# Second layer of a fused network: keys and k by k scores of two batches ahead of all query work

## The chip, the cores and the metric

The kernel runs on one core of one Trainium2 chip. Its time is the device time of one execution in microseconds (us). Three runs of the kernel before are shown: 820.59 us (median), 819.68 and 837.18.

The core has five engines that run side by side, each through its own list of instructions in a fixed order: TensorE (PE, matmuls, with the weight load PEld beside it), VectorE (DVE), ScalarE (ACT), GpSimd (POOL) and SyncE (SP, which here only issues DMAs). They meet through semaphores. TensorE writes to PSUM, eight banks that the other engines read and free.

## The reference

x is 4 batches of 256 tokens by 256 channels. Two layers; each is an attention and a feed-forward network, both on a gated input and added to x. The change touches the attention of the second layer alone. With 16 heads of 16 channels it computes, cut to what matters:

```python
q, k = _rope(q, k)                          # q, k, v, beta from hidden_states
s = einsum('bihd,bjhd->bhij', k, k) * scale # k by k scores, strictly lower
m = max(s, -1); e = where(strict, exp(s - m), 0)
p = e / sum(e, -1)
A = p * beta + eye                          # lower triangular, 256 by 256 a head
u = solve_triangular(A, v, lower=True)
sc = einsum('bihd,bjhd->bhij', q, k) * scale
o = softmax(where(causal, sc, -inf)) @ u
return o @ Wo
```

The triangular system needs keys, values and beta; queries come in only with the last softmax. The feed-forward network behind it routes tokens to eight experts.

## The kernel before, in words

Every engine walks one list of steps, ORDER, made by make_order() (VectorE walks DVE_ORDER, the same list with some steps put a little later by lag()). A step is a tuple, such as ("proj", 1, b, 1): projection in layer 1, batch b, of keys (1) or queries (0). So the place of a step in the list sets the order on each engine; there is no planner. The steps of the second attention for batch b, with the lines of the instructions in the trace:

- gate: tanh on ScalarE (L1273), product on VectorE (L1557): the attention's input.
- proj: fp32 matmuls, then rotary embedding on VectorE (L1575 to L1578). split: three bf16 parts of the result (VectorE, L1587 to L1595), stored to DRAM by SP; for keys SP then loads two stacks, "k" and "kq" (keys in the place of queries); the step qload loads the stack "q".
- vproj: values and beta (TensorE; ScalarE L1298; VectorE L1738).
- kscores, five groups: k by k scores (TensorE), maxima (VectorE L1609 to L1618), exponential with sum (ScalarE L1350). kmax: the maxima are transposed (L1015) and written by four DMAs into the stack (SP, L832). kdiag, den, blocks: diagonal blocks of 32 by 32, transposed (L1760) for GpSimd. kprobs, four groups: the blocks below the diagonal (TensorE, ScalarE L1335).
- On GpSimd, blocks also stands for the inversion of the diagonal blocks: L1985, then 31 pairs of L1992 and L1994. It starts when VectorE has done blocks and the transpose (L1769, step inverse) of the inverse of the batch before.
- solve and update, eight and seven rounds of two halves: the block substitution. A solve is 16 small matmuls and a copy (L1791), an update is 16 matmuls (L1119) and L1777 and L1780 on VectorE. Each waits for the one before: TensorE, VectorE, TensorE.
- scores, eight groups: q by k scores (TensorE), maxima (VectorE L1628, L1629). minus, max: their transposition. probs, eight groups: scores again with the maxima in, exponential (ScalarE L1319, L1320). pv: times u. otr, oT, wo: normalisation and output projection.

proj, vproj, kscores, kdiag, kprobs, scores, probs, pv and others take turns on the two slots of the ring "mid" in PSUM (table RINGS, which also names the engine that frees each slot); a step takes the slot that the step two places before it in that ring has freed.

The list has a part ahead of the first inverse, and four substitutions. spread() deals the steps in ahead[b] (work on other batches) evenly between the rounds of substitution b. Before the change the first part does keys and queries of batches 0, 1 and 2, both batches' k by k scores, and all of batch 0's scores and probs.

## Time and profile before

| | |
|---|---|
| median of the runs | 820.59 us |
| profiled execution, its time | 820.95 us |
| its span | 819.1 us |
| VectorE busy | 555.0 us, 68% |
| TensorE busy | 515.0 us, 63% |
| ScalarE busy | 300.3 us, 37% |
| GpSimd busy | 227.1 us, 28% |
| second attention, from the first requant to its last gate | 313.47 to 650.90 us |

A row of the timeline is start, duration, engine, line, operation, output and input, count, and in brackets how long the engine had been idle before it and who released it. Times are counted from the start of the span. PEclk is the granted clock of TensorE as a share of its full speed. SPq is SP's DMA issue.

### The profile page before, as it was taken

The numbers are of one execution on the slowest core, as the hardware profiler recorded it, in microseconds if no ns is written. First come the engines' busy times: TensorE is split into PE (matmuls) and PEld (weight loads), VectorE is DVE, ScalarE is ACT, GpSimd is POOL, SyncE is SP. The second block draws the span as 40 slices with busy tenths as digits, with TensorE's granted clock in tenths as the row PEclk, the third lists the DMA queues.
The fourth block names the chain that finished last, engine by engine and source line by source line (L and its number), as shares of the span: only waits on it lengthen the run. The fifth ranks groups of instructions, "written<-read, shape, count | busy, mean of one in ns | idle before, by whom it ended". The sixth has DMA issues, their size and how long they took to land. (4 is left out here: it accounts for less than half of the span.)

```text
span 819.1 us, 17908 instructions
## 1 busy us (share of the span) xinstructions
PE 515.0 (63%) x7444; PEld 424.2 (52%) x7444; DVE 555.0 (68%) x1066; ACT 300.3 (37%) x716; POOL 227.1 (28%) x320
## 2 busy tenths in 40 slices
PE   0362555875859554327565676678886750899980
PEld 0352444764648443325443455466655540899980
DVE  6899699797969847766656684663664165667834
ACT  3354333543456340062654204523213150365520
POOL 3000000000000000104848807816830036043254
PEclk9875775986888786755586666687979555899996
DMA  8445041050000100760070150020001162666224
GB/s 307 149 76 116 1 89 28 1 117 1 2 0 2 52 0 17 159 136 5 3 155 6 40 90 7 7 47 7 10 10 12 55 245 85 245 204 235 78 58 136
DMA packets 52067, 61.30 MB, mean 75 GB/s; under 512 B 25409, under 2 KB 45393, under 8 KB 47505
## 3 DMA queue, kind: packets, MB, share of 16 engines
q1 hardware_dynamic: 50176, 55.15, 25.1%
q0 software_dynamic: 1808, 4.99, 2.0%
q8 instruction: 59, 0.97, 0.5%
q14 instruction: 24, 0.19, 0.1%
HBM read 45.24 MB, written 13.63 MB: 72 GB/s over the span
## 5 line engine op out<-in xcount | busy, mean ns | idle before, releaser
L888 PE MATMUL psum<-arena 32*32 32x16 f32 (+18 forms) x5608 | 357.6, 274 | 214.3 <-DVE arena L1557 75.7
L888 PEld LDWEIGHTS psum<-arena 32*32 32x32 f32 (+6 forms) x5608 | 284.4, 128 | 287.1 <-DVE arena L1557 78.4
L1994 POOL TENSOR_TENSOR arena<-arena 128x31 f32<-128x31 f32 (+15 forms) x124 | 68.4, 552 | 9.7
L1992 POOL TENSOR_TENSOR arena<-arena 128x31 f32<-128x31 f32 (+15 forms) x124 | 64.4, 519 | 9.7
L1350 ACT ACTIVATE psum<-psum,arena 128x256 f32<-128x256 f32 (+7 forms) x128 | 45.7, 364 | 30.4 <-DVE arena L1618 30.2
L1527 DVE TENSOR_TENSOR_SCAN arena<-arena 128x255 f32<-128x255 f32 x64 | 42.5, 726 | 11.4 <-ACT arena L1262 11.4
L1628 DVE TENSOR_REDUCE arena<-psum 128x2 f32<-128x512 f32 (+1 forms) x48 | 41.3, 861 | 12.5 <-PE psum L888 11.8
L1972 POOL DMA_DIRECT2D arena<-wq x1 | 0.9, 862 | 171.9 <-PE psum L888 171.9
L1319 ACT ACTIVATE arena<-psum 128x512 f32<-128x512 f32 (+1 forms) x48 | 35.4, 736 | 35.8 <-PE psum L888 35.5
L2005 POOL TENSOR_TENSOR fc_second_parts<-arena,fc_first_parts 128x2048 fp32r<-128x2048 f32 x6 | 27.9, 4650 | 63.7 <-ACT fc_first_parts L1438 63.7
L1262 ACT ACTIVATE arena<-arena 128x255 f32<-128x255 f32 x64 | 27.2, 498 | 46.6 <-DVE arena L1513 46.6
L1425 ACT ACTIVATE psum<-psum,arena 128x256 f32<-128x256 f32 x64 | 24.8, 457 | 48.3 <-PE psum L888 48.3
L1438 ACT ACTIVATE fc_first_parts<-arena 128x2048 fp32r<-128x2048 f32 x16 | 30.4, 1918 | 26.3 <-PE psum L888 26.3
L1119 PE MATMUL psum<-arena 32*32 32x224 f32 (+6 forms) x896 | 38.3, 317 | 2.0 <-issue 1.8
L2012 POOL DMA_INDIRECT dispatched<-arena x16 | 20.3, 1266 | 69.1 <-DVE arena L1845 64.5
L1513 DVE TENSOR_TENSOR_SCAN arena<-arena 128x256 f32<-128x256 f32 x64 | 39.0, 671 | 0.5
L888 PE MATMUL psum<-input_first_parts,fc_first_parts 128*128 128x256 f32 x128 | 37.2, 291 | 2.6 <-DVE input_second_parts L1880 1.5
L888 PE MATMUL psum<-fc_first_parts,hidden_first_parts 128*128 128x256 f32 x128 | 36.9, 288 | 2.7 <-DVE hidden_second_parts L1898 2.7
L888 PE MATMUL psum<-input_second_parts,fc_first_parts 128*128 128x256 f32 x128 | 36.8, 287 | 0.0
L888 PE MATMUL psum<-input_first_parts,fc_second_parts 128*128 128x256 f32 x128 | 36.8, 287 | 0.0
L1777 DVE STREAM_TRANSPOSE arena<-psum 128x64 f32<-128x64 f32 x56 | 13.8, 246 | 33.5 <-PE psum L1119 32.7
L888 PE MATMUL psum<-fc_first_parts,hidden_second_parts 128*128 128x256 f32 x128 | 36.2, 283 | 0.0
(179 smaller groups left out, 928.0 us busy)
## 6 DMA issues: line engine op xcount, KB each, us to landing
arena<-fc SPq DMA_DIRECT2D x16, 1024.0 KB, 5.2
arena<-parts SPq DMA_DIRECT2D x40, 256.0 KB, 4.5
parts<-arena SPq DMA_DIRECT2D x16, 384.0 KB, 3.6
arena<-parts SPq DMA_DIRECT2D x40, 128.0 KB, 5.4
dispatched<-arena SPq DMA_DIRECT2D x1, 2048.0 KB, 18.9
arena<-arena SPq DMA_DIRECT2D x128, 8.0 KB, 1.8
arena<-dispatched SPq DMA_DIRECT2D x8, 256.0 KB, 3.3
expert_rows<-arena SPq DMA_DIRECT2D x8, 256.0 KB, 2.3
```

The source lines that it names most:

```text
L888: return nc.tensor.matmul(out, lhsT, rhs, start=start, stop=stop)
L1119: last = nc.tensor.matmul(acc(half)[rows, qq, (s + 1) * BLK:T], ublk[rows, s, q, :], later[b % 2][s][rows, q, :], start=s == 0 and qq == 0 ...
L1262: A(scan[s + 1][:, ct, 0:T - 1], scan[s][:, ct, 0:T - 1], ACT.Copy, scale=back[:, i:i + 1]).then_inc(scaled, 1)
L1319: step_(A(prob[:, hs, 0:T], hi, ACT.Exp, scale=scale))
L1350: ins = A(s_, s_, ACT.Exp, bias=nbias[:, n:n + 1], accum_out=ncc[b][:, n:n + 1])
L1438: A(w_parts[i][e % 2][0][:], fcw[e % NW][i], ACT.Copy).then_inc(w_first, 1)
L1513: ins = V.tensor_tensor_scan(scan[s][:, ct, :], dd, src[:, ct, bt(b)], 0.0, ALU.mult, ALU.add)
L1527: st(V.tensor_tensor_scan(scan[s][:, ct, T - 2::-1], dd, scan[s + 1][:, ct, T - 2::-1], scan[s][:, ct, T - 1:T], ALU.mult, ALU.add))
L1628: st(V.tensor_reduce(mneg[:, H + j * n:H + (j + 1) * n], hi, axis=AX.X, op=ALU.max, negate=True))
L1992: link(G_.tensor_tensor(tmp, A3[:, k + 1:BLK, k:k + 1].to_broadcast([P, rows, w]), X3[:, k:k + 1, 0:w].to_broadcast([P, rows, w]), ALU.mult))
L1994: ins = G_.tensor_tensor(X3[:, k + 1:BLK, 0:w], X3[:, k + 1:BLK, 0:w], tmp, ALU.add)
L2005: G_.tensor_tensor(second[:], fcw[e % NW][1], first[:].bitcast(F32), ALU.subtract).then_inc(w_second[1], 1)
```

## The change

It rewrites the list. Ahead of the first inverse now stand keys and values of batches 0 and 1, k by k scores, diagonal blocks and kprobs of both (interleaved), the keys of batch 2, and behind them the queries and query scores of batch 0 and the query projection of batch 1. Batch 0's probabilities and batch 2's queries go into substitution 0, batch 3's queries into substitution 1. The step inverse stands at the end of the work dealt into the substitution before. Two waits follow: SP's load of the second "kq" stack waits for two requants in place of four, and GpSimd's fill of the third key stack stands at the first vproj.

```diff
-    o += [("requant", 0), ("gate", 2, 0)] + keys_then_queries(0) + [("qload", 0), ("vproj", 0), ("requant", 1), ("gate", 2, 1)]
-    o += keys_then_queries(1) + [("qload", 1), ("vproj", 1), ("requant", 2), ("requant", 3), ("gate", 2, 2)]
-    o += groups("kscores", 1, 0) + [("kmax", 1, 0)] + groups("scores", 1, 0)[:4] + [("kdiag", 0), ("den", 0), ("blocks", 0)]
-    o += groups("kprobs", 1, 0) + groups("scores", 1, 0)[4:] + [("minus", 1, 0), ("max", 1, 0)]
-    o += groups("kscores", 1, 1) + [("kmax", 1, 1)] + keys_then_queries(2)
-    o += [("kdiag", 1), ("den", 1), ("blocks", 1)] + groups("kprobs", 1, 1) + groups("probs", 1, 0) + [("qload", 2), ("vproj", 2)]
+    def keys(b):
+        return [("proj", 1, b, 1), ("split", 1, b, 1)]
+
+    def asked(b):
+        return [("proj", 1, b, 0), ("split", 1, b, 0)]
+
+    ks, sc, pr = ([groups(kind, 1, b) for b in range(B)] for kind in ("kscores", "scores", "probs"))
+    o += [("requant", 0), ("gate", 2, 0)] + keys(0) + [("vproj", 0), ("requant", 1), ("gate", 2, 1), ("proj", 1, 1, 1)]
+    o += ks[0][:2] + [("split", 1, 1, 1)] + ks[0][2:] + [("kmax", 1, 0), ("requant", 2), ("requant", 3), ("vproj", 1)]
+    o += [("kdiag", 0), ("den", 0), ("blocks", 0), ("gate", 2, 2)] + ks[1][:1] + groups("kprobs", 1, 0)[:2] + ks[1][1:2] + groups("kprobs", 1, 0)[2:]
+    o += ks[1][2:] + [("kmax", 1, 1)] + asked(0) + [("qload", 0)] + [("kdiag", 1), ("den", 1), ("blocks", 1)]
+    o += groups("kprobs", 1, 1) + keys(2) + sc[0] + [("minus", 1, 0), ("max", 1, 0)] + asked(1) + [("qload", 1), ("vproj", 2)]
...
-    ahead = [k2 + [[("gate", 2, 3)], [("proj", 1, 3, 1), ("split", 1, 3, 1)]] + d2 + [[("proj", 1, 3, 0), ("split", 1, 3, 0)], [("vproj", 3)]]
-             + queries(1),
-             k3 + [[("otr", 1, 0)]] + d3 + p1[:3] + [[("oT", 1, 0)]] + p1[3:6] + out(0)[1:] + p1[6:] + [[("qload", 3)]] + queries(2),
...
+    ahead = [one_each(pr[0][:4]) + k2 + [[("gate", 2, 3)]] + one_each(pr[0][4:]) + [keys(3)] + d2 + [asked(2), [("qload", 2), ("vproj", 3)]] + queries(1) + [[("inverse", 1)]],
+             k3 + [[("otr", 1, 0)]] + d3 + p1[:3] + [[("oT", 1, 0)]] + p1[3:6] + out(0)[1:] + p1[6:] + [asked(3), [("qload", 3)]]
+             + queries(2) + [[("inverse", 2)]],
...
+    o += [("inverse", 0)]
...
-        solve = [[("inverse", b), ("solve", b, 0, 0), ("solve", b, 0, 1)]]
+        solve = [[("solve", b, 0, 0), ("solve", b, 0, 1)]]
...
-                                sp.wait_ge(x_ready, 2 * B)
+                                sp.wait_ge(x_ready, B + 2)
...
-                elif kind == "qload" and step[1] == 0:
-                    pool.wait_ge(parts_ready[0], B + 1)
+                elif kind == "vproj" and step[1] == 0:
+                    pool.wait_ge(parts_ready[1], B + 1)
```

The changed file is seven lines longer ahead of the programs, so its lines are seven higher. Three places, in the order of one engine's instructions. First VectorE behind the first gate and key projection of the attention. Before, the split of the keys and then projection (L1575 to L1578) and split of the same batch's queries:

```order
L1595 TENSOR_TENSOR arena<-arena 128x512
L1575 TENSOR_TENSOR arena<-psum,arena 128x512
L1577 TENSOR_TENSOR psum<-psum,arena 128x512
L1578 TENSOR_TENSOR arena<-arena,psum 128x512
L1587 CAST arena<-arena 128x512
```

With the change, from batch 1's gate (L1564) and key projection (L1582 to L1585) on:

```order
L1564 SCALAR_TENSOR_TENSOR arena<-arena 128x2x256
L1582 TENSOR_TENSOR arena<-psum,arena 128x512
L1584 TENSOR_TENSOR psum<-psum,arena 128x512
L1585 TENSOR_TENSOR arena<-arena,psum 128x512
L1616 TENSOR_REDUCE arena<-psum 128x4
L1622 TENSOR_SCALAR arena<-arena 128x4
```

The first k by k scores (L1616) stand right behind the second key projection; before, two query projections, their splits and three requants came first.

Second, TensorE at the start of substitution 0. Before, behind the solve (32x16) come the k by k scores of batch 2 and then the first update (L1119):

```order
L888 MATMUL psum<-arena 32x16 x16
L888 MATMUL psum<-arena 32x256 x4
L888 MATMUL psum<-arena 32x32 x4
...
L1119 MATMUL psum<-arena 32x224 x16
L888 MATMUL psum<-arena 32x32 x32
```

With the change, behind the solve come one group of batch 0's probabilities (128x256, 128x128), the update (L1126), two groups, the next solve, one group and only then k by k scores:

```order
L895 MATMUL psum<-arena 32x16 x16
L895 MATMUL psum<-arena 128x256
L895 MATMUL psum<-arena 128x128
L895 MATMUL psum<-arena 128x256
L895 MATMUL psum<-arena 128x128 x5
L1126 MATMUL psum<-arena 32x224 x16
```

The k by k scores of batch 2 moved behind the first update; before, the first group stood ahead of it.

Third, VectorE in substitution 1, behind the update of round 4. Before, the output's residual (L1670), a gate, the solve's copy (L1791), the next update:

```order
L1780 SCALAR_TENSOR_TENSOR arena<-arena 128x16 x2
L1670 TENSOR_TENSOR arena<-psum,arena 128x2x256
L1557 SCALAR_TENSOR_TENSOR arena<-arena 128x2x256
L1791 COPY arena<-psum 128x2x16 x2
L1777 STREAM_TRANSPOSE arena<-psum 128x64
```

With the change, the copy (L1798), then projection and split of batch 3's queries and one group of scores (L1635, L1636) ahead of the next update:

```order
L1787 SCALAR_TENSOR_TENSOR arena<-arena 128x16 x2
L1798 COPY arena<-psum 128x2x16 x2
L1582 TENSOR_TENSOR arena<-psum,arena 128x512
L1584 TENSOR_TENSOR psum<-psum,arena 128x512
L1585 TENSOR_TENSOR arena<-arena,psum 128x512
L1594 CAST arena<-arena 128x512
L1599 TENSOR_TENSOR arena<-arena 128x512
L1600 CAST arena<-arena 128x512
L1602 TENSOR_TENSOR arena<-arena 128x512
L1635 TENSOR_REDUCE arena<-psum 128x2
L1636 TENSOR_REDUCE arena<-psum 128x2
L1784 STREAM_TRANSPOSE arena<-psum 128x64
```

The pair of projection and split came here from substitution 0; the residual and gate now lie one round earlier.

## Rows read from the trace of the kernel before

**Rows 1.** Stretches between inverse transposes: length; PE, PEld, DVE, ACT, POOL busy; PEclk; DMA.

```profile
313.47:428.12 114.65, 62.72 (x1571) 48.90 (x1571) 74.91 (x143) 44.37 (x169) 41.01 (x67) 0.64 0.38 81
428.12:491.45 63.33, 40.78 (x1081) 29.19 (x1081) 46.13 (x124) 14.31 (x68) 37.72 (x65) 0.66 0.27 50
491.45:556.48 65.03, 45.98 (x1198) 33.99 (x1198) 37.94 (x111) 26.02 (x93) 36.51 (x65) 0.71 0.12 19
556.48:600.73 44.25, 36.60 (x806) 27.77 (x806) 24.84 (x83) 12.70 (x27) 37.01 (x65) 0.81 0.08 9
600.73:650.90 50.17, 36.59 (x713) 26.09 (x713) 17.56 (x67) 11.53 (x23) 0.74 (x1) 0.81 0.07 8
```

**Rows 2.** Waits, 313 to 651 us: who for whom, us in total, times, longest.

```profile
POOL arena L1985 <- DVE arena L1769: 53.0, 3, 23.5
...
DVE arena L1738 <- ACT arena L1298: 8.6, 1, 8.6
```

**Rows 3.** Timeline of GpSimd: starts of the first, second and last inversion.

```profile
378.00 1.91 POOL L1985 TENSOR_TENSOR arena<-arena 128x1024 f32<-128x1024 f32 x1 [44.84 <-DVEq L1762]
...
430.20 1.91 POOL L1985 TENSOR_TENSOR arena<-arena 128x1024 f32<-128x1024 f32 x1 [9.01 <-DVE arena L1769]
...
558.62 1.91 POOL L1985 TENSOR_TENSOR arena<-arena 128x1024 f32<-128x1024 f32 x1 [23.45 <-DVE arena L1769]
```

**Rows 4.** Timeline of VectorE, 339 to 461 us.

```profile
339.70 0.69 DVE L1575 TENSOR_TENSOR arena<-psum,arena 128x512 f32<-128x512 f32 x1 [3.62 <-PE psum L888]
...
344.25 0.69 DVE L1575 TENSOR_TENSOR arena<-psum,arena 128x512 f32<-128x512 f32 x1
...
375.77 0.21 DVE L1759 STREAM_TRANSPOSE arena<-arena 128x32 f32<-128x32 f32 x1 [1.81 <-ACT arena L1328]
...
379.92 0.69 DVE L1628 TENSOR_REDUCE arena<-psum 128x2 f32<-128x512 f32 x1 [2.07 <-PE psum L888]
...
386.71 1.22 DVE L1609 TENSOR_REDUCE arena<-psum 128x4 f32<-128x1024 f32 x1 [1.51 <-PE psum L888]
...
405.37 0.69 DVE L1575 TENSOR_TENSOR arena<-psum,arena 128x512 f32<-128x512 f32 x1 [4.18 <-PE psum L888]
...
410.90 0.69 DVE L1575 TENSOR_TENSOR arena<-psum,arena 128x512 f32<-128x512 f32 x1
...
427.77 0.26 DVE L1738 TENSOR_TENSOR arena<-psum,arena 128x16 f32<-128x16 f32 x2 [8.63 <-ACT arena L1298]
...
460.55 0.34 DVE L1791 COPY arena<-psum 128x32 f32<-128x32 f32 x2 [4.31 <-PE psum L888]
```

**Rows 5.** Stretch of batch 0's k by k exponentials (L1350): length, ScalarE busy, PEclk.

```profile
354.00:368.60 14.60, 11.89 (x64) 0.50 0.61 138
```

**Rows 6.** Groups by line, ScalarE: kprobs' exponentials; busy us, mean ns, idle before.

```profile
L1335 ACT ACTIVATE arena<-psum 128x896 f32<-128x896 f32 (+6 forms) x28 | 14.9, 597 | 5.1 <-PE psum L888 5.1
```

**Rows 7.** Timeline of TensorE's matmuls, 372 to 614 us.

```profile
372.53 2.81 PE L888 MATMUL psum<-arena 98*32 98x32 bf16 x152 [0.34 <-DMA arena<-arena]
...
391.18 1.26 PE L888 MATMUL psum<-arena 96*32 96x64 bf16 x64 [3.40 <-ACT psum L1350]
...
416.80 5.14 PE L888 MATMUL psum<-arena 98*128 98x256 bf16 x40 [0.30 <-ACT arena L1335]
422.21 1.51 PE L888 MATMUL psum<-arena 98*128 98x256 bf16 x16 [0.27 <-ACT arena L1320]
...
431.15 3.13 PE L1119 MATMUL psum<-arena 32*32 32x224 f32 x32
...
452.05 2.36 PE L1119 MATMUL psum<-arena 32*32 32x160 f32 x32
...
606.90 1.72 PE L1119 MATMUL psum<-arena 32*32 32x224 f32 x32 [0.24 <-DVE arena L1791]
...
613.84 1.29 PE L1119 MATMUL psum<-arena 32*32 32x160 f32 x32
```

**Rows 8.** Timeline of SP: the four DMAs of batch 0's key maxima.

```profile
368.68 2.31 SPq L832 DMA_DIRECT2D arena<-arena  x4
```

More of the change, by code:

```diff
@@ L274, in make_order @@
     (k2, d2), (k3, d3) = inverted(2), inverted(3)
-    ahead = [k2 + [[("gate", 2, 3)], [("proj", 1, 3, 1), ("split", 1, 3, 1)]] + d2 + [[("proj", 1, 3, 0), ("split", 1, 3, 0)], [("vproj", 3)]]
-             + queries(1),
-             k3 + [[("otr", 1, 0)]] + d3 + p1[:3] + [[("oT", 1, 0)]] + p1[3:6] + out(0)[1:] + p1[6:] + [[("qload", 3)]] + queries(2),
-             [[("otr", 1, 1)]] + p2[:3] + [[("oT", 1, 1)]] + p2[3:6] + out(1)[1:] + p2[6:] + queries(3),
+    ahead = [one_each(pr[0][:4]) + k2 + [[("gate", 2, 3)]] + one_each(pr[0][4:]) + [keys(3)] + d2 + [asked(2), [("qload", 2), ("vproj", 3)]] + queries(1) + [[("inverse", 1)]],
+             k3 + [[("otr", 1, 0)]] + d3 + p1[:3] + [[("oT", 1, 0)]] + p1[3:6] + out(0)[1:] + p1[6:] + [asked(3), [("qload", 3)]]
+             + queries(2) + [[("inverse", 2)]],
+             [[("otr", 1, 1)]] + p2[:3] + [[("oT", 1, 1)]] + p2[3:6] + out(1)[1:] + p2[6:] + queries(3) + [[("inverse", 3)]],
              [[("otr", 1, 2)]] + p3[:3] + [[("oT", 1, 2)]] + p3[3:6] + out(2)[1:] + p3[6:]]
+    o += [("inverse", 0)]
     for b in range(B):
-        solve = [[("inverse", b), ("solve", b, 0, 0), ("solve", b, 0, 1)]]
+        solve = [[("solve", b, 0, 0), ("solve", b, 0, 1)]]
         for s in range(1, NS):
@@ L317, in lag @@
         chain = step[0] in ("inverse", "update", "solve", "den", "blocks")
-        if step[0] == "inverse":
+        if step[0] == "solve":
             solving = True
```

## The prediction
> **What bounds the kernel now.** I read the stages first. Cut at the four transposes that hand an inverse from GpSimd to the substitution (L1769), the second layer's attention takes 114.65 us up to the first, then 63.33, 65.03, 44.25 and 50.17 us [rows 1]. In none of the first three is one engine full: VectorE is busy for 74.9 of 114.65 us and 46.1 of 63.33, TensorE less, and the granted clock is 0.64, 0.66 and 0.71, so TensorE is mostly at the lower of its two levels. It is a chain that hops between engines.
>
> Then the waits: GpSimd waits 53.0 us in all for L1769 [rows 2]. Its first inverse runs from 378.00 to 421.19 (430.20 less 9.01 of waiting), 43.2 us, and it starts each of the next only when VectorE has come to the transpose in its own order; the last starts at 558.62 [rows 3] and is done as the last transpose starts at 600.73. So GpSimd binds in one stage, 556.48 to 600.73, with 44.25 us. Before that, an earlier inverse is worth nothing by itself: what counts is when VectorE reaches its transposes, at 428.12, 491.45 and 556.48. I therefore forecast those three times; the two stages behind them keep their length, since what the change does there is to swap neighbours.
>
> Last, VectorE's own idle time ahead of 428.12. The largest is 8.63 us at 427.77: TensorE and ScalarE do the eight probability groups of batch 0 and the value projection, and VectorE has nothing. Others: 3.62 us for a projection at 339.70, 1.81 and 2.07 around the diagonal blocks, 1.51 at 386.71, 4.18 at 405.37 [rows 4].
>
> **Stage A, up to the first transpose.** What goes: the 8.6 us behind the probabilities; two waits of 2.1 us in the query scores (one is the 2.07), because all eight groups now stand together with k scores, projections and diagonal long issued; the 1.5 us at 386.71; 3.3 us inside the k scores of batch 0 and before the third key projection, since a split (half of the 4.55 us of a pair, below) now lies inside the first, and part of the 4.18 is hidden at the second. That is 17.6 us. One projection and split (batch 2's queries) leave the stage; from 405.37 to 410.90 [rows 4] such a pair took 5.5 us beside a running inverse. (From 339.70 to 344.25, with GpSimd idle, 4.55.)
>
> What comes: (a) the k scores of batch 1. Now they run from 386.71 to 401.19 (405.37 less 4.18), 14.5 us. ScalarE needs 11.9 us for five such groups, eight blocks of 1.5 [rows 5], and TensorE already waits 3.40 us for it at 391.18 [rows 7], because only two slots of the middle ring exist. The change puts the four kprobs of batch 0 into the same ring between them, each one or two activations of 0.6 us [rows 6], and about as much of TensorE. Walked with these durations (VectorE's part of a group some 2.5 us, then ScalarE's 3.0, then a kprobs, then the slot), the nine steps take 22.3 us, so +7.8. (b) The diagonal of batch 0 now has only two requants and a value projection before it. Its rows are issued by 368.68 and TensorE starts 3.85 us later [rows 7, 8]; with kdiag (most of the 2.81 us of that row) and ScalarE's exponential (about 1) behind it VectorE waits 4.3 us in place of 1.81: +2.5. (c) Both query projections were hidden under the keys' split; alone, each is a wait like the 3.62 or 4.18 at a key projection [rows 4]. I take 3.2 and 3.3: +6.5. (d) The first k scores stand right behind a projection while their stack is loaded: +0.5. Sum +17.3.
>
> So idle time is a draw (-0.3), and with the work that leaves (5.5, less 0.9 that the split of batch 0's queries gains in length, since it now runs beside the inverse as the pair at 405.37 did) stage A is **4.9 us** shorter. Bounds: all of the 8.6 and 5.5 kept (14.1); nothing kept (0).
>
> **Stage B, first substitution.** In: eight probability groups, on TensorE and ScalarE. VectorE's work is the same: batch 2's queries come in, batch 3's go out. Now the first three rounds hide under k scores of batch 2; the gate is done 28.1 us after the transpose (460.55 less 4.31), the copy before the next projection 32.4 us after [rows 4]. With the change the k scores come to VectorE only behind the second update, by my walk some 8 us later, so the first two rounds have nothing on VectorE to cover them. Walked: the gate is done at 32.7 (+4.6). Then round three runs with four probability groups before the projection (at 416.80 five such took 5.14 us [rows 7], 4.1 for four, of which 2 are hidden; solve, update and VectorE's part some 3 more): the projection reaches VectorE 7.5 us later. Behind it one update and solve are missing, -1.5. Sum **+6.0**. The ends are 0 (all in holes of TensorE: it is busy 40.8 of 63.3 us [rows 1]) and 8 x 1.03 = +8.2, or 10 if the projection behind them also waits for its slot. I take the walk, which lies between.
>
> **Stage C, second substitution.** Comes in: batch 3's query projection and split. VectorE's part is 4.55 us with GpSimd idle, as it is there by then (the third inverse takes 43 of the 65 us). TensorE does the projection ahead of the solve that VectorE waits for, 2 to 3 us in which VectorE has only an update left; against that, the update behind is ready when the split ends, about -1.5. **+5.5**, ends 4 and 7.6. SP's new load of batch 3's queries waits for batch 1's last probabilities, which are issued ahead of it, and nobody needs it for 40 us: 0.
>
> **Sum.** -4.9 + 6.0 + 5.5 = +6.6 on the profiled execution's 820.95 us: 827.5. The runs shown have their median 0.36 lower: **827 us**.
>
> **A rule against the sum.** The granted clock is 0.64 to 0.71 up to 556.48 and 0.81 behind it, and prices follow: the first update takes TensorE 3.13 us in substitution 0 and 1.72 in substitution 3, the third 2.36 and 1.29, a probability group 1.03 at 416.80 and 0.75 at 422.21 [rows 1, 7]. If more work in the substitution raised the clock there, the three long updates (second one estimated between: 1.3) would give back 3.8, eight groups 2.2, two projections (by halves of a 3.6 us wait) some 1.8: 7.8 us in all, and the time would be 819. That is rival 2. The Trainium skill, "TensorE: Matmul & The Clock Gate", section "Part 1: The HAM clock gate", says just this: the throttled clock is the default, and activity releases it. By that rule the time is 819, by my rows of today's clock 827; the trace agrees with the rule in that the clock did rise within the block of probabilities, yet there nothing interrupted it, and in the substitution each group is followed by a wait.
>
> **Rivals.** Changes under 2% (16.4 us) can hardly be told from none here.
> 1. *The idle time is really gone*, 20%. The middle ring is no obstacle, stage A gives 14.1 us; B costs 0, C 4.5: -9.6, **811 us**. For it: VectorE is the engine with most work and the hole of 8.6 us is real. Against: the ring's waits for ScalarE [rows 7].
> 2. *The clock rises in stage B*, 18%: **819 us**. For it: the rise at 422.21. Against: above.
> 3. *Exposed probabilities*, 11%: slower. In stage B TensorE's order puts one or two groups before each update, and each waits for a ring slot that ScalarE frees late, as its k scores of batch 2 take 2.9 us a group. Then all rounds stretch: B +10, C +7.6, A gives nothing: +17.6, **838 us**. It decides once VectorE's idle time in stage B passes 27 us (it is 17.2, 63.33 less 46.13). For it: ScalarE is in strict order and gets 16 more activations there. Against: the first four groups come before any k scores.
> 4. *Nothing moves* (the order says otherwise: first k scores ahead of the second split) 1%.
>
> The forecast has 50%. Range 8 in 10: from 811, rival 1's sum, to 836, the forecast with B at 8.2 and C at 7.6 and A at -1 (+14.8); it leaves out rival 3 and the half of rival 1 below its sum. Chances: faster by over 2% (under 804.2) needs more than rival 1's full sum, 3%; slower by over 2% (over 837.0) rival 3, 10%; within, 87%.
>
> **What would show it.** In the profile after: first inverse starts near 362 in place of 378.00 and it changes nothing; VectorE reaches the first L1769 (now seven lines on) at 423, the next at 492 to 493, the third at 563; the k scores of batch 1 stretch over 22 us; the idle time before the first value beta (8.63) is gone; between the first transpose and the end of the gate 32 to 33 us; a projection wait of 2 to 3 us in the second substitution. I am wrong if stage A ends before 418 (rival 1), if stage B is under 64 us at a granted clock over 0.75 (rival 2), or if stages D and E change by over 2 us.

## The result, and the profile after

The changed kernel takes **829.99 us** (median of 4 runs, 826.39 to 833.2) against 820.17 us for the kernel before in the same comparison (also 4 runs): ratio 1.012, 95% interval [1.0068, 1.0173]. It is slower by some 10 us, under 2%. The profiled execution took 829.61 us, with a span of 827.8 us. The forecast was 827.0 us, range 811 to 836. Ratios rest on fast executions alone: one of 837.18 us among the four of the kernel before, and one of 1207.97 us among the six with the kprobs together below, are left out of them.

The stretches of the profile after, cut at the same instructions as [rows 1] (first requant, the four inverse transposes, last gate). The columns are length; PE, PEld, DVE, ACT, POOL busy; PEclk; DMA share; GB/s.

```profile
311.58:426.84 115.26, 56.82 (x1499) 43.58 (x1499) 69.49 (x135) 37.14 (x153) 41.64 (x67) 0.62 0.31 64
426.84:492.78 65.94, 44.21 (x1145) 33.13 (x1145) 46.95 (x123) 21.21 (x84) 37.74 (x65) 0.70 0.35 72
492.78:564.39 71.61, 50.87 (x1206) 37.56 (x1206) 42.13 (x118) 25.79 (x93) 36.56 (x65) 0.67 0.13 24
564.39:609.36 44.97, 36.70 (x805) 27.82 (x805) 24.35 (x83) 12.71 (x27) 37.45 (x66) 0.80 0.08 9
609.36:659.59 50.23, 35.20 (x713) 25.03 (x713) 17.58 (x68) 11.52 (x23) 0.26 (x1) 0.82 0.08 8
```

| stretch | before | after | difference | forecast |
|---|---|---|---|---|
| A, up to the first transpose | 114.65 | 115.26 | +0.6 | -4.9 |
| B, substitution 0 | 63.33 | 65.94 | +2.6 | +6.0 |
| C, substitution 1 | 65.03 | 71.61 | +6.6 | +5.5 |
| D and E | 94.42 | 95.20 | +0.8 | 0 |
| all | 337.43 | 348.01 | +10.6 | +6.6 |

The whole span grew by 8.7, because the first requant came 1.9 us earlier, which the change does not touch. In the kernels built from the changed one below, and in its second profile, it came between 311.5 and 313.4 us, so that is scatter. Stage A has 5.4 us less of VectorE's work than before (69.49 against 74.91) and yet is not shorter: its idle time on VectorE rose from 39.7 to 45.8 us.

VectorE's timeline in stage A, after. Columns as in the rows ahead of the prediction: start, duration, line, operation, and in brackets the idle time before it and its releaser.

```profile
338.44 1.22 DVE L1616 TENSOR_REDUCE arena<-psum 128x4 f32<-128x1024 f32 x1 [2.70 <-PE psum L895]
...
362.66 0.21 DVE L1766 STREAM_TRANSPOSE arena<-arena 128x32 f32<-128x32 f32 x1 [4.69 <-ACT arena L1335]
...
371.95 1.29 DVE L1616 TENSOR_REDUCE arena<-psum 128x4 f32<-128x128 f32 x2 [4.23 <-PE psum L895]
...
379.36 1.29 DVE L1616 TENSOR_REDUCE arena<-psum 128x4 f32<-128x256 f32 x2 [5.24 <-PE psum L895]
...
392.02 0.69 DVE L1582 TENSOR_TENSOR arena<-psum,arena 128x512 f32<-128x512 f32 x1 [4.16 <-PE psum L895]
...
402.36 0.69 DVE L1582 TENSOR_TENSOR arena<-psum,arena 128x512 f32<-128x512 f32 x1 [1.45 <-PE psum L895]
...
408.68 0.69 DVE L1635 TENSOR_REDUCE arena<-psum 128x2 f32<-128x512 f32 x1 [1.62 <-PE psum L895]
...
421.96 0.69 DVE L1582 TENSOR_TENSOR arena<-psum,arena 128x512 f32<-128x512 f32 x1 [3.57 <-PE psum L895]
...
426.51 0.26 DVE L1745 TENSOR_TENSOR arena<-psum,arena 128x16 f32<-128x16 f32 x2
426.86 1.91 DVE L1776 STREAM_TRANSPOSE arena<-arena 128x1024 f32<-128x1024 f32 x1
```

What the reader is to see: the value beta (L1745) ahead of the transpose has no idle time in front, where it had 8.63 us [rows 4]. But two waits of 4.23 and 5.24 us now stand inside the k scores of batch 1, three waits (4.16, 1.45, 3.57) stand ahead of projections that are no longer paired, and 4.69 us stand ahead of the diagonal's transpose. The hole was not closed; it was cut up.

GpSimd, after: the starts of its first, second and last inversion.

```profile
364.83 2.46 POOL L1992 TENSOR_TENSOR arena<-arena 128x1024 f32<-128x1024 f32 x1 [38.09 <-DVEq L1769]
...
428.94 1.91 POOL L1992 TENSOR_TENSOR arena<-arena 128x1024 f32<-128x1024 f32 x1 [20.29 <-DVE arena L1776]
...
566.54 1.91 POOL L1992 TENSOR_TENSOR arena<-arena 128x1024 f32<-128x1024 f32 x1 [29.95 <-DVE arena L1776]
```

The first inversion starts 13.2 us earlier than in [rows 3] (11.3 us earlier, counted from the first requant), and GpSimd then waits 20.29 us, where it waited 9.01. Its waits for the transpose add up to 73.4 us, against 53.0 [rows 2].

### The profile page after: what moved, and what is told of

The parts are those of the page before. It is cut to its first block and busy times, and to the rows that moved or that the text cites. A ratio compares the mean times of both kernels' runs of the same rounds, so it can differ in the third digit from the quotient of the medians.

```text
span 827.8 us, 17909 instructions
## 1 busy us (share of the span) xinstructions
PE 516.4 (62%) x7444; PEld 425.8 (51%) x7444; DVE 554.3 (67%) x1066; ACT 299.8 (36%) x716; POOL 227.3 (27%) x320
## 5 line engine op out<-in xcount | busy, mean ns | idle before, releaser
L895 PE MATMUL psum<-arena 32*32 32x16 f32 (+17 forms) x5608 | 356.3, 277 | 224.2 <-DVE arena L1564 71.2
L895 PEld LDWEIGHTS psum<-arena 128*32 128x32 f32 (+6 forms) x5608 | 282.4, 130 | 297.0 <-DVE arena L1564 73.2
L1357 ACT ACTIVATE psum<-psum,arena 128x256 f32<-128x256 f32 (+7 forms) x128 | 45.8, 375 | 35.8 <-DVE arena L1625 34.3
L1534 DVE TENSOR_TENSOR_SCAN arena<-arena 128x255 f32<-128x255 f32 x64 | 42.5, 726 | 11.3 <-ACT arena L1269 11.3
L1635 DVE TENSOR_REDUCE arena<-psum 128x2 f32<-128x512 f32 (+1 forms) x48 | 41.3, 861 | 10.6 <-PE psum L895 10.0
L1992 POOL TENSOR_TENSOR arena<-arena 128x1024 f32<-128x1024 f32 x4 | 8.2, 2048 | 111.5 <-DVE arena L1776 73.4
L1126 PE MATMUL psum<-arena 32*32 32x224 f32 (+6 forms) x896 | 37.7, 318 | 1.1 <-DVE arena L1798 1.1
```

The source lines that it names most:

```text
L895: return nc.tensor.matmul(out, lhsT, rhs, start=start, stop=stop)
L1126: last = nc.tensor.matmul(acc(half)[rows, qq, (s + 1) * BLK:T], ublk[rows, s, q, :], later[b % 2][s][rows, q, :], start=s == 0 and qq == 0 ...
L1357: ins = A(s_, s_, ACT.Exp, bias=nbias[:, n:n + 1], accum_out=ncc[b][:, n:n + 1])
L1534: st(V.tensor_tensor_scan(scan[s][:, ct, T - 2::-1], dd, scan[s + 1][:, ct, T - 2::-1], scan[s][:, ct, T - 1:T], ALU.mult, ALU.add))
L1635: st(V.tensor_reduce(mneg[:, H + j * n:H + (j + 1) * n], hi, axis=AX.X, op=ALU.max, negate=True))
```

## The experiments

Each was timed beside the kernel before on the same chip; ratios are to that kernel. Stage lengths are of the profiled executions.

### Only the probabilities inside

From the kernel before: batch 0's eight probability groups go into substitution 0, and behind them the load of batch 2's queries (qload), which stood behind them before; nothing else.

```diff
-    o += [("kdiag", 1), ("den", 1), ("blocks", 1)] + groups("kprobs", 1, 1) + groups("probs", 1, 0) + [("qload", 2), ("vproj", 2)]
+    o += [("kdiag", 1), ("den", 1), ("blocks", 1)] + groups("kprobs", 1, 1) + [("vproj", 2)]
-    ahead = [k2 + [[("gate", 2, 3)], [("proj", 1, 3, 1), ("split", 1, 3, 1)]] + d2 + ...
+    p0 = one_each(groups("probs", 1, 0))
+    ahead = [p0[:4] + k2 + [[("gate", 2, 3)]] + p0[4:] + [[("qload", 2)], [("proj", 1, 3, 1), ("split", 1, 3, 1)]] + d2 + ...
```

> The kernel before with one part of the change: batch 0's eight probability groups inside substitution 0 (four ahead of batch 2's k by k scores, four behind the gate), the rest of the list as before. If the hole of 8.6 us ahead of the first transpose is real and substitution 0 takes the groups as cheaply as in the changed kernel (65.94 us in place of 63.33), stage A falls to 106 us, stage B rises to 66, and the time is about 814 us (-6). Rival, the groups are exposed in the substitution (my forecast's +6.0 to +8.2): B 69.5 to 71.5, time 818 to 820.

Measured: **813.86 us**, ratio 0.9931 [0.9907, 0.9954]. Stage A takes 108.04 us (-6.6), B 65.57 (+2.2), C 64.77. Its windows A and B, and VectorE's end of stage A:

```profile
313.50:421.54 108.04, 56.91 (x1507) 44.87 (x1507) 74.98 (x142) 37.59 (x153) 40.94 (x67) 0.61 0.35 77
421.54:487.11 65.57, 42.59 (x1145) 31.61 (x1145) 47.74 (x123) 21.11 (x84) 37.60 (x65) 0.76 0.33 64
```

```profile
421.21 0.26 DVE L1739 TENSOR_TENSOR arena<-psum,arena 128x16 f32<-128x16 f32 x2 [2.11 <-ACT arena L1299]
421.56 1.91 DVE L1770 STREAM_TRANSPOSE arena<-arena 128x1024 f32<-128x1024 f32 x1
```

The 8.63 us hole shrinks to the 2.11 us of the value projection, and eight groups in the substitution cost 2.2. That is 4.4 us of the 6.8 that its second attention is shorter by. Another 2.0 lie in stage E (48.17 us, 50.17 before), where no step moved; E lies between 47.8 and 51.9 us in the profiles of the other experiments, and I did not trace why. This part of the change is a gain of its own, and what loses time in the changed kernel is elsewhere.

### The probabilities taken out again

From the changed kernel: the same step back.

```diff
-    ... + asked(1) + [("qload", 1), ("vproj", 2)]
+    ... + asked(1) + [("qload", 1)] + pr[0] + [("vproj", 2)]
-    ahead = [one_each(pr[0][:4]) + k2 + [[("gate", 2, 3)]] + one_each(pr[0][4:]) + [keys(3)] + d2 + ...
+    ahead = [k2 + [[("gate", 2, 3)]] + [keys(3)] + d2 + ...
```

> The changed kernel with batch 0's eight probability groups back ahead of the first transpose. If moving them in was a gain, stage A grows by 8 (115.3 to about 123) and stage B falls by 2.6 (65.9 to 63.3): 835 us, slower than the changed kernel. Rival, they are what makes the changed kernel slower: B falls by 6 or more, A grows by less than 6, and the time is 830 or less.

Measured: **837.53 us**, ratio 1.0236 [1.0196, 1.0275]. A 122.23 (+7.0 against the change), B 63.06 (-2.9). The hole is back in the same place:

```profile
433.70 0.26 DVE L1745 TENSOR_TENSOR arena<-psum,arena 128x16 f32<-128x16 f32 x2 [8.17 <-ACT arena L1305]
```

Both ways round the move is worth about 7 in stage A and costs 2 to 3 in stage B.

### Batch 3's queries back in substitution 0

From the changed kernel.

```diff
-    ahead = [... + [asked(2), [("qload", 2), ("vproj", 3)]] + queries(1) + [[("inverse", 1)]],
-             k3 + ... + p1[6:] + [asked(3), [("qload", 3)]]
+    ahead = [... + [asked(2), [("qload", 2), ("vproj", 3)], asked(3)] + queries(1) + [[("inverse", 1)]],
+             k3 + ... + p1[6:] + [[("qload", 3)]]
```

> The changed kernel with batch 3's query projection and split back in substitution 0 (behind batch 2's), which then has both. If the pair costs its full length wherever it stands (4.5 us of VectorE plus a wait), stage C falls by 6.6 us (71.6 to 65) and stage B grows by 4.5 to 6.6 (65.9 to 71 or 72): time 828 to 830, no difference. Rival, substitution 0 has holes that hide a part of it: B grows by 2 or less and the time is 825.

Measured: **829.44 us**, ratio 1.0148 [1.0101, 1.0195]; the time of the changed kernel. Its windows B and C:

```profile
424.07:499.35 75.28, 46.77 (x1153) 34.90 (x1153) 50.25 (x130) 21.13 (x84) 38.08 (x65) 0.67 0.34 68
499.35:564.08 64.73, 45.28 (x1198) 33.78 (x1198) 38.72 (x111) 25.99 (x93) 36.39 (x65) 0.71 0.12 20
```

C gives back 6.9 us and is as long as before; B takes 9.3. So the pair of batch 3's queries is the whole +6.6 of stage C, and once stage B holds the eight groups and batch 2's pair, it has no cheaper place there. One wait of the 9.3 can be named: VectorE stood 4.19 us ahead of 483.30, until a store of the split before was done (released by a DMA; SP issued that store at 476.30). The two splits of queries stand directly behind one another there. The rest of the 9.3 was not traced.

### kprobs of batch 0 together, ahead of batch 1's k scores

From the changed kernel: the interleaving in the ring is taken away, all else stays.

```diff
-    o += [("kdiag", 0), ("den", 0), ("blocks", 0), ("gate", 2, 2)] + ks[1][:1] + groups("kprobs", 1, 0)[:2] + ks[1][1:2] + groups("kprobs", 1, 0)[2:]
-    o += ks[1][2:] + [("kmax", 1, 1)] + asked(0) + ...
+    o += [("kdiag", 0), ("den", 0), ("blocks", 0), ("gate", 2, 2)] + groups("kprobs", 1, 0)
+    o += ks[1] + [("kmax", 1, 1)] + asked(0) + ...
```

> The changed kernel with the four kprobs groups of batch 0 together, ahead of batch 1's five k by k score groups, instead of between them. If the interleaving in the two slots of the middle ring costs what I forecast (22.3 us for the block where 14.5 was), the block is now 4 to 5 plus 14.5 = 19 us and stage A falls by 3 (115.3 to 112): 827 us. Rival, the ring's pace is ScalarE's whatever the order (16 us of its work in both): stage A stays within 1 us.

Measured: **824.83 us**, ratio 1.0079 [1.0037, 1.0122]. Stage A 107.48 us: -7.8 against the profile after, -7.0 against the second profile of the same kernel below. TensorE in the block, here:

```profile
364.38 1.80 PE L895 MATMUL psum<-arena 98*32 98x160 bf16 x64 [0.39 <-ACT arena L1342]
366.49 2.28 PE L895 MATMUL psum<-arena 96*32 96x256 bf16 x96 [0.30 <-ACT arena L1342]
372.75 1.26 PE L895 MATMUL psum<-arena 96*32 96x64 bf16 x64 [3.98 <-ACT psum L1357]
375.65 1.26 PE L895 MATMUL psum<-arena 96*32 96x96 bf16 x64 [1.63 <-ACT psum L1357]
379.45 0.72 PE L895 MATMUL psum<-arena 96*32 96x128 bf16 x32 [2.54 <-ACT psum L1357]
```

and in the changed kernel:

```profile
369.81 2.98 PE L895 MATMUL psum<-arena 98*32 98x192 bf16 x128 [6.26 <-ACT psum L1357]
377.18 3.28 PE L895 MATMUL psum<-arena 98*32 98x128 bf16 x160 [4.38 <-ACT psum L1357]
384.98 0.72 PE L895 MATMUL psum<-arena 96*32 96x128 bf16 x32 [4.53 <-ACT psum L1357]
```

Three waits of 6.26, 4.38 and 4.53 us for ScalarE, 15.2 in all, against 8.2. The rows show the kprobs (98 rows) waiting for ScalarE's exponential of a k score (L1357), which frees the slot; by the order of the ring the next k score then waits for the slot of that kprobs, so the engines take turns. From the end of the diagonal's transposes to the last maxima the block lasts 23.2 us, and 16.7 with the kprobs ahead: the interleaving costs 6.5. The k scores alone last 22.3 us interleaved, 14.1 together and 14.5 in the kernel before. A ring with a third slot was not tried, so whether the slots or ScalarE's fixed order sets the pace stays open.

### Where the second split of keys stands

Two kernels, both from the last one. The first puts the split ahead of the k scores of batch 0, while their stack is loaded:

```diff
-    o += ks[0][:2] + [("split", 1, 1, 1)] + ks[0][2:] + [("kmax", 1, 0), ("requant", 2), ("requant", 3), ("vproj", 1)]
+    o += [("split", 1, 1, 1)] + ks[0] + [("kmax", 1, 0), ("requant", 2), ("requant", 3), ("vproj", 1)]
```

> The kernel of the run with kprobs together, and batch 1's split of keys ahead of batch 0's k by k scores instead of between their second and third group, so that it covers the wait for the stacks (VectorE waited 2.92 us there). If that wait was a cost by itself, stage A falls by 2 (107.5 to 105.5) and the time to 822.5. Rival, the split only changes places with it: inside the k scores it filled ScalarE's time, which comes back as a wait there, and stage A stays within 1.3 us (what two profiles of the same stage A differed by).

Measured: **821.29 us**, ratio 1.0013 [0.999, 1.0036], but stage A is 107.27 us, where it was 107.48. The split only changed places: the wait for the first k scores falls from 2.92 to 0.28 us and comes back as 1.55, 0.87 and 1.01 behind the next ones. The median is 3.5 us lower than that of the last experiment, which ran on another chip; the two profiled spans (822.0 and 821.3) do not show a difference, and I leave it unresolved. The profiled execution is the fastest of the last experiment (823.17 us) and one of the slowest of this one (823.78), so the stage lengths cannot show what the medians differ by; that the split only changed places is shown for the profiled execution alone.

The second puts the split behind the rows of maxima:

```diff
+    o += ks[0] + [("kmax", 1, 0), ("split", 1, 1, 1), ("requant", 2), ("requant", 3), ("vproj", 1)]
```

> The kernel of the run with kprobs together, and batch 1's split behind batch 0's key maxima, so that SP issues the four small DMAs of the maxima ahead of the eight loads of batch 1's stacks. TensorE waited 2.62 us for these rows at batch 0's diagonal blocks, 5.0 us after their issue, where the kernel before needed 3.85. If the stack loads held them up, the wait falls below 1 us, the first inversion starts 1.5 to 2 us earlier, and stage A falls by up to 2 (107.5 to 106). Rival, the rows take 5 us whatever stands ahead of them, and nothing falls.

Measured: **828.54 us**, ratio 1.0106 [1.0063, 1.0149], A 113.97. TensorE's waits for DMAs in it:

```profile
357.83 2.57 PE L895 MATMUL psum<-arena 98*32 98x32 bf16 x152 [2.14 <-DMA arena<-arena]
...
371.02 2.29 PE L895 MATMUL psum<-arena 96*32 96x256 bf16 x96 [7.12 <-DMA arena<-parts]
```

The later store and load of batch 1's stack come out as 7.12 us of waiting at its first k scores. SP issued the load from 359.66 on, so TensorE starts 11.4 us behind the first issue; in the kernel with the kprobs together it was issued 17.9 us ahead of its use (348.61, use at 366.49), and no wait showed. The rows of maxima gained little: TensorE starts 4.3 us behind their issue, where it took 5.0 with the stack loads ahead, and its wait is 2.14 us in place of 2.62. The first inversion starts 2.3 us earlier after the first requant, and stage A is 6.5 us longer: the earlier inversion does not make up for the later load.

### An early inversion by itself

Three kernels ask what an earlier inverse is worth, all with the probabilities inside as in the first experiment. One puts batch 0's k scores and diagonal ahead of batch 1's queries:

```diff
-    o += keys_then_queries(1) + [("qload", 1), ("vproj", 1), ("requant", 2), ("requant", 3), ("gate", 2, 2)]
-    o += groups("kscores", 1, 0) + [("kmax", 1, 0)] + groups("scores", 1, 0)[:4] + [("kdiag", 0), ("den", 0), ("blocks", 0)]
+    o += keys_then_queries(1)[:2] + groups("kscores", 1, 0) + [("kmax", 1, 0)] + keys_then_queries(1)[2:] + [("qload", 1)]
+    o += [("kdiag", 0), ("den", 0), ("blocks", 0), ("vproj", 1), ("requant", 2), ("requant", 3), ("gate", 2, 2)]
```

> Meant to beat both kernels: the kernel with only the probabilities moved, where GpSimd's first inversion ended at 421.06 and its transpose started at 421.56, plus batch 0's k by k scores and diagonal ahead of batch 1's queries, values and the last two requants; query projections stay behind their keys' splits, and kprobs are not interleaved with k scores. If the inversion had become the bound, it starts 6 to 9 us earlier and stage A falls by 2 to 4 (108.0 to 104 to 106), time 810 to 812. Rival, the inversion binds nothing, as in the kernel before, and the earlier k scores only bring their waits for loads and rows with them: stage A 108 to 110, time 814 to 816.

Measured: **817.11 us**, ratio 0.9967 [0.9946, 0.9989]; A 111.66, 3.6 us longer than with the probabilities alone. GpSimd's first and second inversion:

```profile
366.97 1.91 POOL L1986 TENSOR_TENSOR arena<-arena 128x1024 f32<-128x1024 f32 x1 [35.63 <-DVEq L1763]
...
425.39 1.91 POOL L1986 TENSOR_TENSOR arena<-arena 128x1024 f32<-128x1024 f32 x1 [15.32 <-DVE arena L1770]
```

It starts early and then waits 15.32 us. The second uses only the requants and values as cover for the diagonal:

```diff
-    o += keys_then_queries(1) + [("qload", 1), ("vproj", 1), ("requant", 2), ("requant", 3), ("gate", 2, 2)]
-    o += groups("kscores", 1, 0) + [("kmax", 1, 0)] + groups("scores", 1, 0)[:4] + [("kdiag", 0), ("den", 0), ("blocks", 0)]
+    o += keys_then_queries(1) + [("qload", 1)]
+    o += groups("kscores", 1, 0) + [("kmax", 1, 0), ("requant", 2), ("requant", 3), ("vproj", 1), ("kdiag", 0), ("den", 0), ("blocks", 0), ("gate", 2, 2)]
```

> The same reordering on the kernel with only the probabilities moved, in which VectorE reached the transpose 0.5 us behind the inversion's end. If VectorE's own order bounds stage A there, an earlier inversion gives nothing and stage A stays within 1.3 us of 108.0, time 814. Rival: the reordering itself saves VectorE waits and stage A falls by 2 or more.

Measured: **815.77 us**, ratio 0.9935 [0.9906, 0.9965], A 108.61. The inversion starts at 371.65, and GpSimd waits 6.40 us behind it; nothing is gained over 108.04.

### Queries one batch later

From the first experiment: batch 2's queries into substitution 0, batch 3's into substitution 1, as in the change, but with stage A's old order.

```diff
-    o += groups("kscores", 1, 1) + [("kmax", 1, 1)] + keys_then_queries(2)
+    o += groups("kscores", 1, 1) + [("kmax", 1, 1)] + keys_then_queries(2)[:2]
-    ... + d2 + [[("proj", 1, 3, 0), ("split", 1, 3, 0)], [("vproj", 3)]]
+    ... + d2 + [keys_then_queries(2)[2:], [("qload", 2), ("vproj", 3)]]
-    ... + p1[6:] + [[("qload", 3)]] + queries(2),
+    ... + p1[6:] + [keys_then_queries(3)[2:], [("qload", 3)]] + queries(2),
```

> The kernel with only the probabilities moved, plus the other moved work alone: batch 2's queries from stage A into substitution 0, batch 3's from substitution 0 into substitution 1. If a pair costs 4.5 to 7 us in each stage and little of it is hidden: stage A 108.0 to 103, B unchanged at 65.6, C 64.8 to 71.5, time 815.5. If the first inversion binds stage A (it ended 0.5 us ahead of its transpose), A stays at 107 to 108, and the whole 6.9 us of stage C is lost: 820.

Measured: **815.83 us**, ratio 0.9945 [0.9917, 0.9972]. A 106.89, C 68.69 (+3.9 over the first experiment). Here, for once, the transpose waits for GpSimd:

```profile
419.16 1.91 DVE L1770 STREAM_TRANSPOSE arena<-arena 128x1024 f32<-128x1024 f32 x1 [3.93 <-POOL arena L1995]
```

So an earlier inversion should pay here, up to 3.9 us. A is only 1.2 us shorter than in the first experiment, where one projection and split less had promised 5; the inversion now holds the transpose back. The requants as cover once more, on this kernel (the same edit as above):

> On the kernel of the run with the queries one stage later, where the first transpose waited 3.93 us for the inversion: batch 0's k by k scores stand ahead of the last two requants and batch 1's values, which then cover the wait for the maxima's rows; the eight query score groups stand together behind the inversion's start. If the inversion's start (376.64) now bounds stage A, it starts 5 to 8 us earlier and stage A falls from 106.9 to 103, time 812. Rival: the k scores stand earlier but VectorE's own order is as long, new waits take the place, and stage A stays at 106 to 108.

Measured: **813.16 us** (5 runs, 812.97 to 817.46), ratio 0.9907 [0.9876, 0.9939]. A is 105.64 us, 1.3 shorter, and the wait has turned round again: GpSimd waits 2.68 us for VectorE. The profiled execution was the slowest of the five (817.46 us), and 1.3 us is within what stage A scatters by (below), so the gain in A is not shown. This and the first experiment (0.9931 [0.9907, 0.9954]) have the two lowest ratios of the study; the intervals of both overlap with each other and with the two kernels in between (0.9935 and 0.9945), so which of the four is fastest stays open. All four beat the kernel before and the changed one.

### The changed kernel once more

> The changed kernel once more, for a second profile: how far the lengths of its stages repeat. Two kernels with the same order in stage A had 115.3 and 112.6 us there. If that is scatter from run to run, this one lies anywhere between 112 and 116; the block of batch 1's k by k scores, which took 22.4 and 22.2, repeats within 0.3 us.

Measured: one execution of 831.03 us. A 114.52, B 66.41, C 71.70, D 44.18, E 50.78. The k scores of batch 1 lasted 22.2 us, as foreseen. Stage A of three profiled executions with the same order there (this, the change, batch 3's queries back) is 112.6 to 115.3 us, so differences under about 2.7 us in stage A between single profiles say little. The changed kernel's own +0.6 in stage A is the upper end of that: by the other two it would be -2.0 and -0.1.

## Why the prediction was right, and where its steps were not

**The mechanism.** As forecast, an earlier first inverse is worth nothing while VectorE comes to the transpose later than it; the three times at which VectorE reaches its transposes decide. Forecast 423, 492 to 493 and 563; measured 426.84, 492.78 and 564.39. The inversion started at 364.83 (forecast 362) and GpSimd waited 20.29 us behind it; two experiments that did only this gained nothing or lost 3.6 us. Only with the probabilities and then batch 2's queries out of stage A's old order did the transpose wait for GpSimd (3.93 us). Stages D and E changed by 0.8 us, inside the bound of 2.

**What goes from stage A.** The 8.6 us: right, and shown both ways. The waits that were to shrink at batch 0's query scores did (behind the 1.62 us ahead of the first, at 408.68, the groups wait 0.34 us at most).

**(a) Ring interleaving, +7.8.** The k scores of batch 1 last from 365.55 to 387.86, 22.3 us, the walked length; taking the interleaving away shortens the block by 6.5. It is the largest single cost in stage A. The edit on the list that looked most like free overlap was the one that cost most.

**(b) The diagonal, +2.5.** VectorE waited 4.69 us, forecast 4.3. The rows of maxima were issued at 353.68 and TensorE started at 359.43, 5.75 us later in place of the 3.85 of [rows 7, 8]. Kdiag and the exponential behind it took 3.23 us up to the transpose, as before (3.24). That the wait grew by only 0.4 over the forecast is partly luck: VectorE had 4.29 us of work behind the issue, where 3.85, 3.2 and a wait of 4.3 leave about 2.8 for it. SP and TensorE, after:

```profile
347.42 3.56 SPq L791 DMA_DIRECT2D arena<-parts  x8
353.68 2.31 SPq L839 DMA_DIRECT2D arena<-arena  x4
```

```profile
337.16 2.28 PE L895 MATMUL psum<-arena 96*32 96x256 bf16 x96 [3.68 <-DMA arena<-parts]
...
359.43 3.03 PE L895 MATMUL psum<-arena 98*32 98x32 bf16 x168 [3.37 <-DMA arena<-arena]
...
407.33 9.04 PE L895 MATMUL psum<-arena 96*128 96x256 bf16 x64 [5.00 <-DMA arena<-parts]
```

**(c) Exposed query projections, +6.5.** 4.16 and 3.57, together 7.7: +1.2 more.

**(d) The first stack load, +0.5: mis-sized.** VectorE waited 2.70 us. The loads were issued from 326.46 to 330.02, and TensorE could start at 337.16, 10.7 us behind the first issue. I had counted a projection and a gate as its cover and not held issue and landing against them.

**A load that the sum left out.** The split of batch 0's queries ends at 397.6; SP issues stack "q" from 400.79, and TensorE starts the query scores at 407.33, after 5.00 us. Before, requants, values and k scores stood between that split and its use. The third key projection and its split cover most of it; VectorE waits 1.62 us.

**What stage A adds up to.** VectorE's work fell by 5.4 us (forecast 4.6), its idle time rose by 6.0 where I had a fall of 0.3. So 6.3 us of idle time are missing from the forecast. Named are 2.2 in (d), 0.4 in (b), 1.2 in (c), 1.6 at stack "q", 0.9 at the second value beta, and 1.8 at the last k scores of batch 0, part of the 3.3 that were to go: 8.1 in all, so 1.8 came in smaller elsewhere, which I did not trace. About half of what is named (4.2 us: (d), (b) and stack "q") is data that moved close to its use. By the second profile and by the kernel with batch 3's queries back the miss in stage A would be 4.8 and 2.9 us in place of 5.5, so the small terms are not sure one by one. From the first requant, the inversion was forecast at 48.5 us (362 less 313.47) and came at 53.3, the transpose at 109.8 and came at 115.3: nearly all of it is lost before the inversion starts.

**Stage B, +6.0: too much.** It was +2.6, and +2.2 with the probabilities alone. VectorE and TensorE, behind the transpose:

```profile
432.11 0.25 DVE L1784 STREAM_TRANSPOSE arena<-psum 128x64 f32<-128x64 f32 x1 [2.54 <-PE psum L1126]
...
437.30 0.25 DVE L1784 STREAM_TRANSPOSE arena<-psum 128x64 f32<-128x64 f32 x1 [2.15 <-PE psum L1126]
...
456.00 1.15 DVE L1564 SCALAR_TENSOR_TENSOR arena<-arena 128x512 f32<-128x512 f32 x1 [0.67 <-ACT arena L1280]
...
463.85 0.69 DVE L1582 TENSOR_TENSOR arena<-psum,arena 128x512 f32<-128x512 f32 x1 [1.82 <-PE psum L895]
```

```profile
430.32 2.91 PE L1126 MATMUL psum<-arena 32*32 32x224 f32 x32
...
436.38 1.50 PE L1126 MATMUL psum<-arena 32*32 32x192 f32 x32
...
451.42 2.36 PE L1126 MATMUL psum<-arena 32*32 32x160 f32 x32
```

The same places before, VectorE's waits for the first three updates and TensorE's second:

```profile
432.83 0.25 DVE L1777 STREAM_TRANSPOSE arena<-psum 128x64 f32<-128x64 f32 x1 [2.01 <-PE psum L1119]
...
444.97 0.25 DVE L1777 STREAM_TRANSPOSE arena<-psum 128x64 f32<-128x64 f32 x1 [2.31 <-PE psum L1119]
...
453.41 0.25 DVE L1777 STREAM_TRANSPOSE arena<-psum 128x64 f32<-128x64 f32 x1 [1.62 <-PE psum L1119]
```

```profile
443.40 2.79 PE L1119 MATMUL psum<-arena 32*32 32x192 f32 x32
```

The gate is done at 457.15, 30.3 us behind the transpose, +2.2 in place of +4.6; this is the step that failed. Its premise, that before the change the first three rounds hide under the k scores of batch 2, does not hold: VectorE waited 2.01, 2.31 and 1.62 us for the three updates there. Ahead of the second, TensorE had k scores that themselves waited 3.40 and 1.97 us for a slot. After, it waits 2.54 and 2.15 us, and at the third, which the k scores now cover, not at all. So there was little cover to lose. From the gate to the projection it was +2.1 more (36.99 us behind the transpose, before 32.68), forecast +2.9; behind it -1.7, forecast -1.5. So the terms behind the gate held.

Rival 2 is not the main thing, but it is there in part. The granted clock of the stage rose from 0.66 to 0.70, and up to the gate from 0.62 to 0.71; that is, TensorE spent more of it at the upper level of 2.4 GHz. The second update stands right behind probability groups now and took 1.50 us in place of 2.79. It took 2.79 again when the groups were taken out, and 1.50 in every kernel that had them in. That is 1.3 of the 3.8 us that rival 2 asked of the three long updates, and by an estimate from these rows about half of the 2.4 us by which the gate came earlier than forecast. The first took 2.91 us (3.13 before, 2.5 to 3.2 in the other kernels), the third 2.36 as before [rows 7], and the fourth 1.93, where it took 1.28. With the probabilities alone the clock was 0.76 and the stage 65.57 us, 0.4 less, not the 64 of rival 2. The Trainium skill, "TensorE: Matmul & The Clock Gate", section "Part 1: The HAM clock gate", says that activity releases the throttled clock. The trace agrees as to direction in this stage, while stage C, with more matmuls than before (1206 against 1198), fell from 0.71 to 0.67.

**Stage C, +5.5.** It was +6.6, and taking the pair out gives 6.9 back. The projection and split take VectorE 4.5 us (546.17 to 550.68) with no wait ahead; the rest is that the chain of solve and update stands still meanwhile.

```profile
545.90 0.35 DVE L1798 COPY arena<-psum 128x32 f32<-128x32 f32 x2 [1.18 <-PE psum L895]
546.17 0.68 DVE L1582 TENSOR_TENSOR arena<-psum,arena 128x512 f32<-128x512 f32 x1
...
550.72 0.69 DVE L1635 TENSOR_REDUCE arena<-psum 128x2 f32<-128x512 f32 x1
...
551.66 0.24 DVE L1784 STREAM_TRANSPOSE arena<-psum 128x64 f32<-128x64 f32 x1
```

The copy that TensorE's next update waits for ends at 546.25, and VectorE comes to that update at 551.66, 5.4 us later. The round before, with a residual and a gate between (copy until 541.40, update fetched at 543.48), took 2.1. The forecast had a wait of 2 to 3 us for the solve behind this projection. It stands at the copy, with 1.18 us (the copy of the same round before, at 542.02, did not wait), so that term was too large by 1 to 2 us; what the stage cost more than forecast lies in the stalled chain.

**The sum.** The profiled execution was forecast at 827.5 us and took 829.61, 2.1 more: A was 5.5 too low, B 3.4 too high, C 1.1 and D with E 0.8 too low, and the first requant came 1.9 us earlier. (The medians, 827.0 and 829.99, differ by 3.) Within a few us the total was right because errors cancel, not because each step was right: that is luck. So is part of the match of the transposes at 492.78 and 564.39: counted from the first requant they came 1.7 to 2.7 and 3.3 us later than forecast. Rival 1 (idle time really gone) fell with stage A, rival 3 with stage B: VectorE's idle time there is 19.0 us (65.94 less 46.95), under its 27.

## What to carry to other kernels

Where several engines hand work on through a two-slot ring, putting a second kind of step between the first kind need not be overlap (here it cost 6.5 us): walk the slots first. Moving a step nearer to its producer exposes the load between them; count from the issue to the landing, with what is queued ahead. And a resource that will wait anyway (here the inversion) gains nothing from starting earlier: do first the one move that closes a hole, here the probabilities alone, which gave 0.9931, and time it apart from the rest. Before pricing a cover as lost, look whether it covers today: waits for the same producer in the trace before say that it does not.

## What the runs showed of the hardware, not expected

- Four small writes (the rows of maxima) took from issue to TensorE's start 3.6 us where the last of eight stack loads had been issued 8 us ahead, 3.85 in the kernel before, 4.3 with stack loads issued behind them, and 5.0 and 5.75 where the last of eight stack loads had been issued 2.7 us ahead (5.6 to 5.9 in three more profiles with the changed order).
- VectorE's requant passes of 0.49 and 0.43 us took 1.80 and 1.14 us where two GpSimd MEMSETs of 1.80 and 1.11 us ran beside them. It is in the kernel before as well and so is no part of the result. In the kernel with batch 0's diagonal ahead of batch 1's queries another requant took 1.76 and 1.14 us, beside the first operations of the inversion (the very first 1.91 us). VectorE and GpSimd in the changed kernel:

```profile
324.05 1.80 DVE L1731 TENSOR_SCALAR arena<-arena 128x512 f32<-128x512 f32 x1
```

```profile
323.76 1.80 POOL L1942 MEMSET arena<- 2x2048 f32 x1 [12.58 <-DVE arena L1602]
```
